# Two-layer graph network on one core: the fused stage's f32 tiles added as two 64-row halves, and each span's batches run as a loop on TensorE

## The reference

```
for l in range(3):                                     # first network
    m = x @ weight[l]
    agg = segment_sum(m[src] * edge_weight[:, None], dst, N)
    x = gru_cell(agg, x, w_ih, w_hh, b_ih, b_hh)
x = layernorm(x0 + x)
for W, b in ((W0, b0), (W1, b1), (W2, b2)):            # second network
    x = relu((x + segment_sum(x[src], dst, N)) @ W.T + b)
x = layernorm(x1 + x)
```

## Time and profile before

| | |
|---|---|
| median of three runs | 3098.06 us (3097.5 to 3099.9) |
| the profiled execution: time, span | 3116.43 us, 3114.7 us |
| TensorE matmuls busy | 3055.5 us, 98% of the span |
| VectorE / ScalarE / GpSimd busy | 36% / 29% / 9% |
| mean granted TensorE clock | 0.997 |

### The profile page before, as it was taken

How to read it: one execution, slowest core, us unless ns; L and a number is a source line. 1 busy time by engine, 2 the same in 40 slices (tenths; PEclk the granted TensorE clock), 3 DMA queues, 4 the chain that set the end, 5 groups by cost and what they waited for, 6 DMA issues and landing times.

```text
span 3114.7 us, 74296 instructions
## 1 busy us (share of the span) xinstructions
PE 3055.5 (98%) x29956; PEld 1975.7 (63%) x29956; DVE 1107.2 (36%) x3061; ACT 909.9 (29%) x2123; POOL 291.1 (9%) x500
## 2 busy tenths in 40 slices
PE   5999999999999999999999999999999999999998
PEld 4788888888888865555555555555555555555554
DVE  5788888888888600000001010111130010001111
ACT  5666666666666510000001010011130010001111
POOL 3222222222222200000000000000000000000000
PEclk9999999999999999999999999999999999999999
DMA  5565555555555587677676777676658777786884
GB/s 183 211 248 246 224 224 246 246 234 224 237 247 240 224 331 273 264 287 279 265 274 251 280 282 282 262 269 272 258 201 332 294 288 280 298 304 260 306 310 164
DMA packets 135446, 809.63 MB, mean 260 GB/s; under 512 B 7972, under 2 KB 17432, under 8 KB 120776
## 3 DMA queue, kind: packets, MB, share of 16 engines
q1 hardware_dynamic: 129704, 800.52, 65.5%
q0 software_dynamic: 4368, 7.97, 0.9%
q10 hardware_dynamic: 1296, 0.01, 0.0%
HBM read 566.04 MB, written 242.44 MB: 260 GB/s over the span
## 4 chain that ended last, share of the span: by engine, by line
PE 98%; issue 1%; DMA 0%; DVE 0%; ACT 0%; POOL 0%; DVEq 0%; POOLq 0%; ACTq 0%
PE ps L758 33%; PE ps L924 25%; PE ps L1003 19%; PE ps L996 11%; PE ps L768 1%; PE ps L769 1%; PE ps L1029 1%; PE ps L746 1%; PE ps L1030 1%; PE ps L771 1%; PE ps L770 1%; PE ps L903 1%; PE ps L1075 0%; PE ps L892 0%; PE ps L1031 0%
## 5 line engine op out<-in xcount | busy, mean ns | idle before, releaser
L758 PE MATMUL ps<-ring,Y 128*128 128x448 f32 x2744 | 1035.7, 539 | 0.0
L758 PEld LDWEIGHTS ps<-ring,Y 128*128 128x128 f32 x2744 | 521.1, 190 | 508.8 <-issue 508.8
L924 PE MATMUL ps<-ring,Y 128*128 128x448 f16 x4116 | 780.6, 352 | 0.0
L1364 ACT ACTIVATE ring<-ps 128x392 f16<-128x392 f32 (+1 forms) x1568 | 654.1, 505 | 303.0 <-PE ps L996 298.0
L924 PEld LDWEIGHTS ps<-ring,Y 128*128 128x128 f16 x4116 | 402.7, 98 | 373.8
L1003 PE MATMUL ps<-ring,Y 128*128 (+1 forms) x2720 | 610.3, 367 | 0.4 <-ACT shared L1326 0.4
L1003 PEld LDWEIGHTS ps<-ring,Y 128*128 128x128 f32 x2720 | 487.1, 190 | 15.5 <-ACT shared L1326 0.8
L996 PEld LDWEIGHTS ps<-shared 64*128 64x128 bf16 x18816 | 337.3, 94 | 129.2 <-ACT ring L1364 82.1
L996 PE MATMUL ps<-shared 64*128 64x49 bf16 (+1 forms) x18816 | 386.7, 190 | 19.3 <-issue 16.3
L1717 DVE TENSOR_TENSOR shared<-shared 128x400 bf16<-128x400 bf16 x1176 | 396.4, 391 | 0.0
L1433 DVE SCALAR_TENSOR_TENSOR shared<-ps,bhh,shared 128x448 f32<-128x448 f32 x28 | 19.1, 684 | 775.4 <-ACT shared L1151 775.4
(11 more groups left out here) (151 smaller groups left out, 1234.7 us busy)
## 6 DMA issues: line engine op xcount, KB each, us to landing
ring<-adj_w SPq DMA_DIRECT2D x84, 2688.0 KB, 8.9
adj_w<-ring SPq DMA_DIRECT2D x56, 2744.0 KB, 12.2
ring<-adj_h SPq DMA_DIRECT2D x42, 2800.0 KB, 9.4
ring<-adj_h SPq DMA_DIRECT2D x42, 2688.0 KB, 9.1
ring<-adj_w SPq DMA_DIRECT2D x28, 2912.0 KB, 9.5
adj_h<-ring SPq DMA_DIRECT2D x56, 1372.0 KB, 5.0
x_keep<-xT SPq DMA_DIRECT2D x1, 3136.0 KB, 10.7
shared<-x_keep SPq DMA_DIRECT2D x1, 3136.0 KB, 15.4
```

The source lines that it names most:

```text
L758: mm = pe.matmul(ps[:, bank, 0:GW], Y[:, h, :], ring[:, s, :, h - h0, :], start=(h == 0), stop=(last and h == TILES - 1))
L924: mm = pe.matmul(ps[:, par, 0:GW], part[:, h, :], ring_h[:, par, s, :, h - h0, :], start=(h == 0 and part is Y_high), stop=(h == TILES - 1 ...
L1364: act.activation(strip[:, :, c0:c0 + UNIT * WIN].rearrange("p h (d j) -> p d h j", d=WIN), psum_unit(a)[:, :, kind, :, :].rearrange("p d j ...
```

## The change

On TensorE, the 64-row form is used for all 49 tiles of every span: `add_tiles` issues two half matmuls for each tile, rows 0 to 63 into bank 4 and rows 64 to 127 into bank 5. The two halves of the aggregate are copied apart by ScalarE (two ACTIVATEs in `fused_evac`), and `fused_gates` multiplies both, 9 f32 matmuls in place of 6. VectorE's addition of the halves is gone.

The half form has its `slot` as a constant, so the body of a span is written twice, for slot 0 and slot 1. The 14 batches of a span are now a loop of 7 passes `j` with two batches `b` in each. Which tile group follows batch 2j+b is picked by nested comparisons of `j` on the sequencer (`pick_group`); the gates and the transposition stand under a comparison each. Spans 2 to 27 (26 spans) run in this form, span 1 is still written out. The banks of the setup, of the columns and of the gates are moved about; the column bank is now shared with a gates bank, and the transposition waits for VectorE's `s_fgv`.

```diff
             def add_tiles(slot, lo, hi):
                 for h in range(lo, hi):
-                    mm = pe.matmul(ps[:, AGG_BANK, 0:SPAN], Y[:, h, :],
-                                   strip_w[:, bass.ds(slot, 1), :, h, :].rearrange("p o b c -> p (o b) c"),
-                                   start=(h == 0), stop=(h == TILES - 1))
+                    for rows, bank in zip(ROW_HALVES, AGG_BANKS):
+                        mm = pe.matmul(ps[:, bank, 0:SPAN], Y[rows, h, :], strip_w[rows, slot, :, h, :],
+                                       start=(h == 0), stop=(h == TILES - 1))
...
             def fused_gates(n):
...
-                for c in range(2):
-                    half = ps[:, RZ_BANK, c * SPAN:(c + 1) * SPAN]
-                    pe.matmul(half, wT[:, c, :], agg_span, start=True, stop=False)
-                    pe.matmul(half, wT[:, 3 + c, :], xg, start=False, stop=True)
-                pe.matmul(ps[:, IH_BANK, 0:SPAN], wT[:, 2, :], agg_span, start=True, stop=True)
-                pe.matmul(ps[:, IH_BANK, SPAN:2 * SPAN], wT[:, 5, :], xg, start=True, stop=True).then_inc(s_fgate, 1)
+                pe.matmul(ps[:, IH_BANK, SPAN:2 * SPAN], wT[:, 5, :], xg, start=True, stop=True)
+                pe.matmul(r_z[0], wT[:, 3, :], xg, start=True, stop=False)
+                pe.wait_ge(s_fev, START + 2 * (n + 1))
+                for a in agg_spans:
+                    pe.matmul(r_z[0], wT[:, 0, :], a, start=False, stop=(a is agg_spans[1]))
+                pe.matmul(r_z[1], wT[:, 4, :], xg, start=True, stop=False)
+                for a in agg_spans:
+                    pe.matmul(r_z[1], wT[:, 1, :], a, start=False, stop=(a is agg_spans[1]))
+                for a in agg_spans:
+                    mm = pe.matmul(ps[:, IH_BANK, 0:SPAN], wT[:, 2, :], a, start=(a is agg_spans[0]),
+                                   stop=(a is agg_spans[1]))
+                mm.then_inc(s_fgate, 1)
...
+            def pick_group(t, slot, j, b, lo, hi):
+                if hi - lo == 1:
+                    if BUFS * lo + b >= FIRST_BATCH:
+                        tile_group(t, slot, BUFS * lo + b)
+                    return
+                mid = (lo + hi) // 2
+                with pe.If(j < mid):
+                    pick_group(t, slot, j, b, lo, mid)
+                with pe.Else():
+                    pick_group(t, slot, j, b, mid, hi)
+
+            def looped_span(t, slot, n_gates):
+                pe.wait_ge(s_cola, t + 1)
+                pe.sem_inc(s_mark_pe, 1)
+                with pe.Fori(0, BATCHES // BUFS) as j:
+                    for b in range(BUFS):
+                        n = BATCHES * t + BUFS * j + b
+                        if b == TRANSPOSE_AT % BUFS:
+                            with pe.If(j == TRANSPOSE_AT // BUFS):
+                                pe.wait_ge(s_fgv, START + GV * n_gates + 2)
+                                slots_to_partitions(t + 1)
+                        if b == GATES_AT % BUFS:
+                            with pe.If(j == GATES_AT // BUFS):
+                                fused_gates(n_gates)
+                        pe.wait_ge(s_hot, HOT * (n + 1))
+                        for a in range(UNITS):
+                            build_unit(n, b, a)
+                        pick_group(t, slot, j, b, 0, BATCHES // BUFS)
...
             with pe.Fori(0, GATHERS // 2 - 1) as i:
-                with pe.Fori(0, 2) as slot:
-                    build_span(2 * i + slot + 2, slot, 2 * i + slot)
...
+                for slot in range(2):
+                    looped_span(2 * i + slot + 2, slot, 2 * i + slot)
...
-                act.activation(by_unit(agg_span), natural(ps[:, AGG_BANK, 0:SPAN]), ACT.Copy).then_inc(s_fev, 1)
+                for agg_span, bank in zip(agg_spans, AGG_BANKS):
+                    act.activation(by_unit(agg_span), natural(ps[:, bank, 0:SPAN]), ACT.Copy).then_inc(s_fev, 1)
```

## The result

The changed kernel takes 3210.43 us (median of 4 runs, 3209.87 to 3211.27) against 3098.51 us of the kernel before (4 runs, 3097.5 to 3099.9). The ratio is 1.0361, with a 95% interval of 1.0343 to 1.0379: 112 us slower. Forecast were 3193 us, between 3078 and 3238, with 0.80 for slower.

A forecast was written before the change was run, and what follows sets the result against it. The prediction took TensorE's own matmul time, busy 98% of the span, as the bound. Its terms summed to +3.65 us a span, +95 us over 26 spans, on 3098 us: 3193 us, range 3078 to 3238.

The forecast's parts named there:

- Term 1: Switches between 128-row and 64-row modes on TensorE: -1.3 us a span at 13 group ends, +0.2 us at the transposition.
- Term 2: The gates on TensorE: 18 records in place of 12, +1.1 us a span.
- Term 3: Sequencer comparisons ahead of each tile group, less a lead of about 0.4 us: +2.9 us a span, the deciding term.
- hidden: Rival: comparisons ahead of groups are covered by the sequencer's lead; -34 us, 3064 us; chance 15%.
- short-jump price: Rival: a taken comparison over one group costs only 0.19 us, so slower by less, 3110 to 3165 us; chance 20%.
- Term 4: First pass, no group behind batch 0: comparisons, jumps and register instructions ahead of the gates are exposed, +0.6 us a span.
- Term 5: Sequencer work behind a group, 0.7 to 1.3 us, mostly covered by the group; a little left, +0.15 us a span.
- instruction fetches: Rival: jumps in the loop make one fetch in each pass, +182 us beside the rest, 3375 us; chance 5%.

The follow-up runs named there:

- before_cmp1: The kernel before with one comparison of the slot, its body empty, ahead of each tile group of the looped spans: 3099.6 us, ratio 1.0003.
- linear_chain: The changed kernel with pick_group asking for j = 0, then j = 1 and so on, in place of halving: 3329.79 us, ratio 1.0745 to the kernel before.
- before_cmp3: The kernel before with three comparisons of the slot, their bodies empty, ahead of each tile group of the looped spans: 3190.73 us, ratio 1.0295.
- two_passes_moved: halves_two_passes with 90 semaphore increments that nobody waits for at TensorE's start: 3072.16 us against 3099.78 of the kernel before, ratio 0.9912.
- looped_whole: The changed kernel's loop and comparisons with whole 128-row tiles, one bank, one ScalarE copy, 6 gate products: 3185.84 us, ratio 1.0225 to the kernel before.
- one_more_compare: The changed kernel with an always true comparison around pick_group, which was folded away, leaving the changed kernel: 3221.73 us, ratio 1.0339 to the kernel before.
- halves_two_passes: The kernel before with all tiles as halves, batches 2 to 13 as two passes of six, two comparisons per group, VectorE adding banks: 3331.68 us, ratio 1.0753.

## Why the prediction was right, and what it missed

The sum can be tested term by term, by the times from start to start of TensorE's matmuls, added up over a looped span (us). The column of before_cmp1 stands for the kernel before, without stalls inside its batches; on those see the end of this section. 0.19 us behind the transposition and 0.285 us behind the gates are the same in all and left out.

| per span | before_cmp1 | changed | linear_chain | before_cmp3 | two_passes_moved |
|---|---|---|---|---|---|
| whole span | 36.28 | 40.04 | 44.61 | 39.81 | 35.12 |
| batch to group, 13 times | 1.46 | 4.33 | 8.95 | 5.09 | 1.41 |
| group to batch, 12 times | 3.42 | 2.46 | 2.53 | 3.42 | 2.19 |
| batch to gates | 0.11 | 0.66 | 0.52 | 0.11 | 0.11 |
| inside the gates | 2.19 | 3.32 | 3.32 | 2.19 | 2.19 |
| group to transposition, and inside it | 0.38 | 0.53 | 0.53 | 0.38 | 0.53 |
| inside batches and groups | 28.24 | 28.28 | 28.29 | 28.15 | 28.23 |

*Term 1, the row modes (forecast -1.3 and +0.2).* From a group to the next batch it is 0.285 us before (3.42 / 12), and 0.182 us in two_passes_moved (2.19 / 12), where nothing else is in the way. So the switch costs 0.10 us, as the prediction read it from the earlier trace rows. There are 12 such ends, not 13, since the transposition stands behind one: -1.23 us. The transposition's part is +0.14. The halves themselves cost nothing, as said: the insides of batches and groups differ by 0.04 us.

*Term 2, the gates (forecast +1.1).* 3.32 - 2.19 = 1.13.

*Term 3, the comparisons (forecast +2.9).* 4.33 - 1.46 = 2.87. This is the term that decided, and both of its parts hold: the size of the steps and what of them is hidden. The price: conditions that are taken have records of 202 to 208 ns, as the earlier trace rows had it for the loop. The lead: one comparison is free, three are not. In linear_chain the same rule forecast +120 us over the changed kernel, and 118 came. So the rival "hidden" fell for the reason given against it, and "short-jump price" because a jump over one group is as dear as one over the whole loop. By the Trainium skill's prices (Advanced Engine Details and Errata, Control Flow Timing), about 108 ns for a compare-and-branch, the changed kernel would have been faster. The trace has 65 to 77 ns when it isn't taken and 202 to 208 when it is, and the measurement decides.

*Term 4, the first pass (forecast +0.6).* 0.66 - 0.11 = 0.55. An unconditional jump, whose price I took as 0.13 us between 0 and 0.27, is a record of 169 ns on the sequencer:

```profile
L1057 PEldq COMPARE_BRANCH  x96: 169/169/169, 220.4 to 1155.0; - x96
```

*Term 5, behind a group (forecast +0.15).* From a group to the next batch the changed kernel has 0.205 us (2.46 / 12), where 0.182 are the array's own: 12 x 0.023 = 0.28 us, about twice the forecast. The timeline of weight loads shows it behind a span's last group, ahead of batch 0:

```profile
366.79 0.85 PEld L996 LDWEIGHTS ps<-shared 64*128 64x128 bf16 x48 [0.32 <-issue]
```

-1.23 + 0.14 + 1.13 + 2.87 + 0.55 + 0.28 and the 0.04 inside the groups make 3.78. The span itself went from 36.28 to 40.04 us, 3.76 us where the sum had 3.65. Times 26 that is 97.8 us; 95 were forecast, 112 came. **What the sum left out** is some 14 us, and it isn't in the steady spans:

- *The first pass through the new code, +11.5 us.* The first two looped spans take longer than two later ones. The windows of these two, of the changed kernel and of before_cmp1:

```profile
109.80:205.40 95.60, 81.05 (x1800) 72.58 (x1794) 64.92 (x181) 51.61 (x128) 18.99 (x32) 0.93 0.45 183
```

```profile
109.30:185.90 76.60, 73.79 (x1590) 64.69 (x1583) 64.66 (x180) 50.93 (x125) 19.83 (x32) 1.00 0.56 229
```

 That is 95.60 - 2 x 40.04 = 15.5 us of excess against 76.60 - 2 x 36.28 = 4.0 us. Two branches of `pick_group` in this stretch have records that no later one comes near (0.21 us at most between 205 and 1170 us):

```profile
L1055 PEldq COMPARE_BRANCH  x1: 4336/4336/4336, 112.3 to 112.3; - x1
L1055 PEldq COMPARE_BRANCH  x1: 3830/3830/3830, 167.3 to 167.3; - x1
```

 Both lie in the first passes. q8 has 8 packets between 100 and 206 us, and none between 210 and 1000, so the likely reason is that these jumps meet code that isn't yet on the chip. The array stood for 4.7 us ahead of the first gates, from 112.4 to 117.1 us, and the granted clock fell to half, the level of 1.2 GHz, while it stood:

```profile
114.80:121.60 6.80, 4.52 (x12) 4.13 (x13) 1.07 (x4) 0.00 (x0) 0.57 (x2) 0.50 1.08 456
```

 So the 15.5 us are 9.6 us more idle time (95.60 - 81.05 against 2 x 2.49) and 6.0 us of matmuls that took longer (81.05 against 2 x 37.55). looped_whole has the same comparisons, but no branch over 0.32 us here, and its clock didn't fall:

```profile
109.30:191.20 81.90, 75.28 (x1596) 64.56 (x1588) 64.80 (x180) 51.05 (x125) 19.11 (x32) 1.00 0.52 213
```

 Its excess is 81.90 - 2 x 39.68 = 2.5 us. Why its jumps wait for nothing and those of the changed kernel do was not settled. With it the 36 us between looped_whole and one_more_compare come out: 26 x (40.40 - 39.68) = 19 us in steady spans, 13 us in the first two (96.0 - 2 x 40.40 = 15.2, less 2.5), and some 3 us each before the loop and behind it. Of the 19 us, 9 are the changed kernel's own second level: one_more_compare has 0.35 us a span more than the changed kernel.
- *The stage's end, some 2 us.* From the loop's end to the end of the span it is 2043.2 us (3209.5 - 1166.3) against 2041.3 (3098.0 - 1056.7) in before_cmp1. The prediction let the last gates, +2.2 us, cancel against span 1. The gates came, the gain of span 1 didn't: the loops begin at 109.8 and 109.3 us.

The third omission is in the base. The profiled execution of before takes 3116.43 us, the runs beside it 3098, and I carried the difference along as a constant. It lies in the batches. In that execution the array stops inside some of them, here in batch 12 of a span:

```profile
332.37 0.90 PE L996 MATMUL ps<-shared 64*128 64x98 bf16 x44
333.49 0.23 PE L996 MATMUL ps<-shared 64*128 64x49 bf16 x4 [0.21 <-issue]
```

Such stops add up to 0.54 us a span (36.82 against 36.28), 26 x 0.54 = 14 of the 18 us. before_cmp1's trace, from a set where before takes 3098.69 us, has none. That is also why the spans are 40.04 us and not the 40.5 that the prediction named: the changed kernel has no such stops, and 36.28 + 3.76 = 40.04. The changed kernel has two levels too, 3211.5 and 3221.7 us, but there the difference lies ahead of groups (4.55 us a span in place of 4.33) and behind them (2.55 in place of 2.45). What makes the one or the other in a set of runs is open.

The rival "instruction fetches", which had 5% and 3375 us, doesn't hold for the changed kernel, but four neighbours of it were just there, at 3305 to 3341 us. The reason given against it, that the body is shorter than before's, was not enough by itself: halves_two_passes is shorter too. In that the forecast had luck: nothing in it looked at where the body begins.

## What to carry to other kernels

Conditions on TensorE's sequencer were free here only while the array still had work queued. Behind the small bf16 matmuls some 0.3 us were hidden: one comparison, taken or not, or two that aren't taken. Three taken ones set the group back by 0.48 us. Behind f32 groups the sequencer's work, by the prediction's estimate 0.7 to 1.3 us, was nearly hidden; so place a comparison behind the long matmuls, or pick with one or two and write the rest out. Then look at q8 inside the loop: a body that just fits may stop fitting when it is moved by some instructions, and that cost over three times as much as the comparisons (252 us against 26 x 2.87 = 75). A form that is slower as part of a change can still be worth having: the changed kernel, with halves and 9 gate products, was 36 us slower than the same loop with whole tiles, while halves with 6 gate products and two comparisons were 28 us faster than before.

## What the runs showed of the hardware

- A branch of TensorE's sequencer has a record of 65 to 77 ns when it isn't taken, 202 to 208 ns when it is, and 169 ns for an unconditional jump. Over one group it is as dear as over a loop.
- The end of a 128-row f32 group ahead of 64-row bf16 matmuls costs 0.285 us from start to start (before_cmp1), the end of a 64-row group 0.182 us (two_passes_moved). At the group's start it is 0.11 us from 64 rows to 128 in before_cmp1 (1.46 / 13), and 0.02 us from 64 rows to 64 in two_passes_moved, where neither of the two comparisons is taken.
- The granted clock was at 0.50 from 114.8 to 121.6 us in the changed kernel, where the array had stopped at 112.4 us, and a loop with fetches in every pass ran at a mean of 0.93 (halves_two_passes) where the same loop without them had 1.00.
- A loop's body that fetched in every pass stopped doing so when it was moved by 90 instructions: 3331.7 against 3072.2 us. In the seven kernels of the table and this one, bodies over at most 7 blocks of 256 instructions stayed on the chip, and those over 8 or more didn't. Only one pair was made to test it; the block's size, where a block begins and the limit are read from these cases.
